# Grouping VectorE's products differently in a three-layer interaction network: ten operations a turn where there were thirteen

## What is computed

```python
x0 = xk = e
for W in (W0, W1, W2):                       # W: 32 x (32 or 64) x 64
    xk = relu(einsum('bmd,bhd,mhk->bkd', x0, xk, W))
    outs.append(sum(xk, axis=2))
h = concat([z, dense_ctx]); h = relu(h @ W_top1 + b_top1)
h = relu(h @ W_top2 + b_top2); y = h @ W_top3
```

## Time and profile before

| | before |
|---|---|
| median of 3 runs | 1191.82 us (1191.45 to 1193.62) |
| the profiled execution: its own time | 1192.97 us |
| its span, first to last instruction | 1191.2 us |
| mean granted TensorE clock | 0.991 of full speed |
| TensorE matmul busy | 1121.3 us (94%) |
| VectorE busy | 1118.8 us (94%) |
| GpSimd busy | 918.8 us (77%) |
| ScalarE busy | 733.9 us (62%) |

### The profile page before, as it was taken

The page is one execution under the profiler, slowest core; times in us unless marked ns, Lnnn a source line. Parts: engine busy times, 40 slices in busy tenths (PEclk is TensorE's granted clock), DMA queues, the critical chain, the costliest instruction groups (busy, mean ns, idle before and its releaser), DMA issues.

```text
span 1191.2 us, 14658 instructions
## 1 busy us (share of the span) xinstructions
PE 1121.3 (94%) x5312; PEld 393.6 (33%) x5312; DVE 1118.8 (94%) x521; ACT 733.9 (62%) x1361; POOL 918.8 (77%) x640
## 2 busy tenths in 40 slices
PE   0488899999999999999999999999999999999997
PEld 0122223333333333333333333333333333333333
DVE  0487999999999999999999999999999999999995
ACT  0343666676667667665766766576676657657653
POOL 6688888888888888888888888888888888885400
PEclk9888999999999999999999999999999999999999
DMA  5887787667678766677876666788666778876300
GB/s 110 190 176 146 158 171 155 138 132 144 140 157 171 157 141 141 132 144 150 172 163 136 143 134 145 144 171 168 139 140 134 143 145 169 166 144 144 61 1 1
DMA packets 76216, 167.25 MB, mean 140 GB/s; under 512 B 21776, under 2 KB 39072, under 8 KB 76144
## 3 DMA queue, kind: packets, MB, share of 16 engines
q1 hardware_dynamic: 59216, 161.95, 64.8%
q0 software_dynamic: 16384, 4.23, 3.6%
q10 hardware_dynamic: 544, 0.14, 0.1%
HBM read 157.86 MB, written 8.40 MB: 140 GB/s over the span
## 4 chain that ended last, share of the span: by engine, by line
PE 86%; POOL 3%; DVE 3%; DMA 3%; issue 3%; ACT 1%; SPq 1%; DVEq 0%
PE acc L600 80%; POOL x_rows L254 3%; DVE p_dve L516 3%; PE acc L672 3%; PE acc L658 1%; PE acc L660 1%; DMA q_tile<-x_of_steps 1%; ACT xb L317 1%; DMA x_rows<-in_table,ids_s 1%; PE acc L680 1%; DMA spread<-x_of_steps 1%; SPq L192 1%; DMA x_of_steps<-x_rows 0%; SPq L219 0%; DVE z L543 0%
## 5 line engine op out<-in xcount | busy, mean ns | idle before, releaser
L600 PE MATMUL acc<-p_dve,w_s 128*64 128x512 f32 x3840 | 863.2, 598 | 22.5 <-DVE p_dve L516 21.8
L254 POOL DMA_INDIRECT x_rows<-in_table,ids_s x512 | 493.7, 964 | 146.1 <-issue 131.2
L516 DVE TENSOR_TENSOR p_dve<-spread,xb 128x3072 f32<-128x3072 f32 (+2 forms) x224 | 572.2, 2682 | 2.9 <-issue 2.9
L516 DVE TENSOR_TENSOR p_dve<-spread,xa 128x2048 f32<-128x2048 f32 (+1 forms) x192 | 501.5, 2730 | 16.6 <-issue 9.1
L600 PEld LDWEIGHTS acc<-p_dve,w_s 128*64 128x64 f32 x3840 | 267.9, 137 | 571.5 <-issue 467.2
L317 ACT ACTIVATE xb<-acc 32x512 f32<-32x512 f32 x512 | 288.8, 564 | 71.6 <-DVE p_dve L516 65.5
L266 POOL TENSOR_TENSOR p_l<-spread,q_tile 128x2048 f32<-128x2048 f32 x60 | 272.7, 4573 | 11.0 <-DMA q_tile<-x_of_steps 10.4
L308 ACT ACTIVATE xa<-acc 64x512 f32<-64x512 f32 x256 | 145.9, 570 | 189.6 <-PE acc L600 155.0
L277 POOL TENSOR_TENSOR p_pool<-spread,x_s 128x1024 f32<-128x1024 f32 x64 | 152.2, 2378 | 94.7 <-PE acc L600 45.9
L600 PE MATMUL acc<-p_l,w_s 128*64 128x512 f32 (+1 forms) x640 | 152.5, 612 | 41.6 <-DVE p_l L556 41.6
L326 ACT ACTIVATE x_s<-acc 64x512 f32<-64x512 f32 x256 | 151.5, 592 | 8.3 <-ACT y_row L449 4.8
(11 more groups left out here) (18 smaller groups left out, 151.1 us busy)
## 6 DMA issues: line engine op xcount, KB each, us to landing
spread<-x_of_steps SPq DMA_DIRECT2D x248, 512.0 KB, 17.4
q_tile<-x_of_steps SPq DMA_DIRECT2D x128, 128.0 KB, 11.4
x_rows<-in_table,ids_s POOLq DMA_INDIRECT x512
x_of_steps<-x_rows SPq DMA_DIRECT2D x64, 128.0 KB
spread<-x_of_steps SPq DMA_DIRECT2D x16, 256.0 KB, 5.4
w_s<-in_w SPq DMA_DIRECT2D x2, 512.0 KB, 5.7
wt<-in_w_top SPq DMA_DIRECT2D x1, 512.0 KB, 6.5
z_all<-in_dense_t ACTq DMA_DIRECT2D x16, 8.0 KB, 8.2
```

The lines of the kernel that those rows point to most:

```text
L254: nc.gpsimd.indirect_dma_start(out=x_rows[:, s % 2, i * DIM:(i + 1) * DIM], out_offset=None, in_=table, in_offset=bass.IndirectOffsetOnAxi ...
L516: nc.vector.tensor_tensor(p_dve[:, to:to + n, :], spread[:, s % 3, tile:tile + n, :], over(x[:], n), ALU.mult).then_inc(dve_made, n)
L600: last = nc.tensor.matmul(acc[b * K:(b + 1) * K, :], w, prod[:, b * BLK:(b + 1) * BLK], start=start, stop=stop)
```

## The change

The table of groups changes, and with it how VectorE cuts its operations. In a regular turn layer 1 goes from groups of 3, 2, 2, 3, 3, 2 chunks to 3, 2, 2, 4, 4; layer 2 from 2, 3, 2, 3, 1, 2, 2 to 3, 4, 3, 3, 2. Step 0's layer 1, which begins at place 0, takes the table of layer 2, and the last layer 2, which begins at place 5, takes that of layer 1.

```diff
-GROUPS_L1 = [(0, 3), (3, 2), (5, 2), (8, 3), (11, 3), (14, 2)]
-GROUPS_L2 = [(0, 2), (2, 3), (5, 2), (8, 3), (11, 1), (12, 2), (14, 2)]
+GROUPS_L1 = [(0, 3), (3, 2), (5, 2), (8, 4), (12, 4)]
+GROUPS_L2 = [(0, 3), (3, 4), (8, 3), (11, 3), (14, 2)]
...
-                for c, n in GROUPS_L1:
+                for c, n in GROUPS_L1 if s > 0 else GROUPS_L2:
...
-            for c, n in GROUPS_L2:
+            for c, n in GROUPS_L1:
                 if c == NT:
                     sums(STEPS - 2, 1)
                     sums(STEPS - 2, 2)
-                if c == CL - 2:
+                if c == GROUPS_L1[-1][0]:
                     sums(STEPS - 1, 1)
                 layer2(STEPS - 1, c, n)
```

## The result

The changed kernel takes 1206.22 us (median of four runs, 1205.72 to 1206.60) against 1191.63 (1191.42 to 1193.62) for the kernel before: a ratio of 1.0116, 95% interval 1.0101 to 1.0131. It is slower by 14.6 us, the forecast was 12, the range was 1198 to 1210. The profiled execution took 1206.04 us, with a span of 1204.2.

A forecast was written before the change was run, and what follows sets the result against it. VectorE was taken to set the pace at 34.61 us a turn; a loop through late chunk 3, TensorE and the ring makes it 35.03. 29 turns at 0.42 are 12.2 us, rounded to 12: 1203.8 us, range 1198 to 1210.

The forecast's parts named there:

- The bound: Regular turns of the kernel before: VectorE sets the pace at 34.61 us a turn, TensorE very close behind.
- TensorE's 34.53: TensorE's own work in a regular turn, about 34.53 us, below which it can't go.
- The saving: VectorE's regular turn: 0.06 us per operation, three fewer save 0.19 us, VectorE alone from 34.61 to 34.42.
- The loop: From layer 2's late chunk 3 through TensorE's first layer and the ring back to VectorE's layer 1: turn of 35.03 us.
- the handoff from TensorE back to VectorE: Ring place freed by TensorE to VectorE's layer 1 start: taken as 0.10 us, bounds nothing and 0.19.
- The check on the kernel before: The same loop summed with the old groups: 33.90 us, 0.7 short of the turn, matching the spare times.
- the second return through layer 2's last operation: VectorE also waits before layer 2's chunks 14 and 15, whose last place comes free when chunk 4 is used.
- The waits: Each turn: TensorE waits 0.1 to 0.9 us before layer 2's chunk 3, VectorE idles twice for 0.2 to 0.4.
- Start, end and loads: Ahead of 138 us, the last layer 2, and `load_a`'s later release: costed at nothing, the start within half a microsecond.
- The saving alone: Rival: VectorE runs without a wait, the ring's spare places absorbing late chunk 3; 1189.4 us, or down to 1186.3; chance 0.06.
- The cancelling case: Rival: the ring's places come free before the matmul records end, loop 34.6 us, time 1191.8; chance 0.04.
- The costlier waits: Rival: VectorE's operations after its two waits a turn lose 0.2 us each, turn 35.4, time 1215; chance 0.10.

The follow-up runs named there:

- e3: The changed kernel with layer 2's operation of four chunks cut into two and two, eleven operations a turn: 1188.78 us, 0.9970 of the kernel before.
- e5: The changed kernel with, on TensorE alone, the first layer's five chunks put after chunk 2 of layer 2, not chunk 3: 1189.09 us, 0.9969 of before.
- e6: The changed kernel with layer 1's first two operations cut 2 and 3 chunks instead of 3 and 2: 1199.29 us, 1.0052 of before.
- e7: The kernel before with the load of `spread`'s first tiles held until layer 2's 13th chunk, not the 11th: 1192.89 us, 1.0002 of before.
- e1: Layer 1 in the changed kernel's five groups, layer 2 in the seven of the kernel before: 1192.50 us, 0.9999 of before.
- e2: Layer 1 in the six groups of the kernel before, layer 2 in the changed kernel's five: 1209.64 us, 1.0138 of before.

## Why the prediction was right

**The bound.** VectorE sets the pace with TensorE close behind: both held. The prediction said that the turn can't go below TensorE's 34.53. That is right for the long run only: the mean turns of e3 and e5 are 34.50 and 34.49, since VectorE can run ahead of TensorE as far as the places of the ring allow, and only the late turns of both come to 34.53 on average.

**The saving.** 0.06 us per operation was right (e3: two fewer, 0.13 less a turn). It did not decide the result, since the loop and no longer VectorE's work set the pace. By the Trainium skill's PSUM figure (Perfetto Trace Analysis, Optimizing Scalar/DVE Operations) two operations fewer would be, as an estimate, 0.25 us, and e3's turn 34.36; the measured 34.48 fits the SBUF figure of that section.

**The loop.** 35.03 forecast, 35.09 measured. All its terms but one were from rows. The one that no row showed, the handoff from TensorE back to VectorE, can be read now: chunk 8 ends at 536.67 + 2.62 + 1.03 = 540.32 and layer 1 starts at 540.47, so 0.15 us, where 0.10 was taken from ScalarE's handoff and the bounds were 0 and 0.19. That is most of the difference. The choice of 0.10 rested on no row with these two engines, and its closeness is in part luck; by the bounds the turn would have been 34.93 to 35.12, so the direction did not hang on it. The check on the kernel before (33.90 by the loop's sum, 0.7 short of the turn) gave the sum its weight, and e6 shows the part of it that the prediction only described, the second return through layer 2's last operation.

**The waits.** Forecast were 0.1 to 0.9 us before chunk 3 and two idle times of 0.2 to 0.4 on VectorE. Measured were 0.68 in one turn and about 0.2 in the other, and 0.17 and 0.32; the text's "about a microsecond" was too much.

**Start, end and loads.** Costed at nothing; the profile shows 0.7 us less at the start, which is within what kernels with equal groups differ by, and 0.2 less at the end, and e7 no effect of the loads. Of the 2.4 us by which the median exceeds the forecast, the span makes up 1.0 (1204.2 against 1203.2). Most of the rest is that the forecast took the profiled execution to lie 1.15 above the median, as it had before, where it now lies 0.2 below.

**The rivals.** The saving alone (1186 to 1189) is what e3 and e5 show once the loop is cut, so its mechanism was real and its condition, the loop under 34.53, was not met. The cancelling case needed a loop of 34.6, and it is 35.09. The costlier waits (1215) didn't come: an operation after a wait starts 0.12 to 0.15 us after the chunk is used, and loses nothing more.

## What to carry to other kernels

Where a consumer follows a producer through a ring, an operation's size is a signal's lateness as well as an overhead: before merging operations, add up the loop from a late signal through the consumer and the ring's free place back to the same operation, and compare it with the period. Here the loop was 0.7 us short of a 34.6 us period, less than one chunk's 1.07, and the merge lengthened it by 1.13. Where the merge is wanted all the same, giving the consumer other work at the spot where it would wait can be worth as much as cutting the operation again.

## What the runs showed of the hardware

**The clock at the end.** Between its last groups of matmuls TensorE waits for ScalarE (1.97, 1.23 and 0.71 us), and in some runs it is granted the lower clock for them. The last stretch of e7_loads_later and of the changed kernel (columns as in the earlier trace rows):

```profile
1180.00:1191.90 11.90, 7.02 (x36) 5.76 (x36) 0.46 (x1) 2.54 (x9) 0.00 (x0) 0.62 0.00 0
```

```profile
1194.00:1204.20 10.20, 4.70 (x36) 3.97 (x36) 0.69 (x1) 2.97 (x10) 0.00 (x0) 1.00 0.00 0
```

The granted clock was 0.62 against 1.00, for the same 36 records after the same idle times: in e7 a part of them ran at 1.2 GHz and not at 2.4. The 16 records of the second of those products took 3.78 us there:

```profile
1184.53 3.78 PE L672 MATMUL acc<-h,wt 128*128 128x128 f32 x16 [1.23 <-ACT h L430]
```

where they take 2.05 at full clock. From the start of the last regular layer 2 to the end of the span it is 49.3 us in the kernel before and 49.1 in the changed kernel, with 1.00, but 51.4 in e7, 51.7 in e1 (0.71 in its last 12.4 us), and 52.6 and 52.8 in e2 and e6 (0.53 in their last 12 us). e7 has the groups of before, so at least its 2 us are not the groups' doing; what decides whether the clock falls there is not shown. The gains of e3 and e5 are 3 us, so this is a reason to read turns and not single times.

**The tail of an operation.** A VectorE operation's record grows while operations follow each other without a wait, from 3.35 us for three chunks early to 3.54 late, though their starts stay 3.26 apart. In the changed kernel, which waits twice a turn, the records keep their short form, and the mean of the 64 on `xb` is 3350 ns; in the kernel before it is 3440:

```profile
L517 DVE TENSOR_TENSOR p_dve<-spread,xb 128x3072 f32<-128x3072 f32 x64 | 211.7, 3350 | 0.8 <-ACT xb L318 0.8
```

The consumer sees the longer one. In the kernel before, the operation on chunks 2 to 4 ends its record at 489.94 (3.42 us long) and at 1043.81 (3.52), and TensorE starts chunk 2 at 489.99 and 1043.86, 0.05 us later both times. The loop was thus some 0.1 us shorter than a mean duration of the kernel before would have made it, and the duration after a wait was the right one to take.
